# Two-layer graph network on one core: chunks of two rows, messages stored as three bf16 parts, tables cleared during the sort

## The reference, cut to what matters

```python
# x [12500, 32], src, dst [400000] (sorted by dst), edge_attr [400000, 16], edge_weight [400000]
def layer0(h, attr, src, dst):
    edge_mats = (attr @ W_bond + b_bond).reshape(-1, 32, 32)      # one 32x32 matrix per edge
    for _ in range(4):
        msg = einsum('eij,ej->ei', edge_mats, h[dst])             # neighbour: dst
        agg = segment_sum(msg, src, num_segments=12500)           # target: src
        h = gru_cell(agg, h, W_ih, W_hh, b_ih, b_hh)
    return h
def layer1(h, src, dst, edge_weight):
    deg = segment_sum(1, dst);  d = where(deg > 0, rsqrt(deg), 0)
    return segment_sum(h[src] * (d[src] * edge_weight * d[dst])[:, None], dst)
x = x + layer0(relu(layernorm(x)), edge_attr, src, dst)
x = x + layer1(relu(layernorm(x)), src, dst, edge_weight)
```

## Time and profile before

| | us |
|---|---|
| median of three runs | 27440.27 (27435.75 to 27440.9) |
| the profiled execution, its own time | 27437.25 |
| its span, first to last instruction | 27435.5 |
| GpSimd busy | 19769.8, 72% of the span |
| TensorE busy | 12435.2, 45% |
| VectorE busy | 10408.2, 38% |
| ScalarE busy | 4649.9, 17% |
| mean granted clock of TensorE | 0.69 of 2.4 GHz |

### The profile page before, as it was taken

How to read it: one execution, slowest core, us unless ns; L and a number is a source line. 1 busy time by engine, 2 the same in 40 slices (tenths; PEclk the granted TensorE clock), 3 DMA queues, 4 the chain that set the end, 5 groups by cost and what they waited for, 6 DMA issues and landing times. The chain is left out here.

```text
span 27435.5 us, 248655 instructions
## 1 busy us (share of the span) xinstructions
PE 12435.2 (45%) x67848; PEld 9433.8 (34%) x67849; DVE 10408.2 (38%) x18376; ACT 4649.9 (17%) x9970; POOL 19769.8 (72%) x20823
## 2 busy tenths in 40 slices
PE   6666664555555455555455555545555530000004
PEld 5444443344443334334334334333434420000004
DVE  9999995333323323333333333333333330000007
ACT  5333332111111111111111111111111110000004
POOL 2777777777777777777677777777777767777771
PEclk5777776777777677777677777767777765555555
DMA  5333332111111111111111111111111121121113
GB/s 206 93 93 95 92 93 52 29 28 28 28 28 27 28 28 29 29 28 28 26 28 28 28 28 29 27 28 29 28 28 28 28 34 44 45 45 44 44 41 91
DMA packets 1814384, 1246.56 MB, mean 45 GB/s; under 512 B 1182629, under 2 KB 1744754, under 8 KB 1789679
## 3 DMA queue, kind: packets, MB, share of 16 engines
q1 hardware_dynamic: 583936, 850.03, 10.4%
q0 software_dynamic: 666016, 324.92, 8.7%
q10 hardware_dynamic: 564300, 70.11, 1.6%
HBM read 957.69 MB, written 285.80 MB: 45 GB/s over the span
## 5 line engine op out<-in xcount | busy, mean ns | idle before, releaser
L1087 POOL DMA_INDIRECT h_rows<-h_table,rec x13680 | 12906.7, 943 | 4242.1 <-issue 4126.8
L1276 PE MATMUL outer<-a_masked,h_by_quarter 128*128 128x136 f32 x27360 | 5298.9, 366 | 8604.9 <-DVE h_by_quarter L1131 8604.9
L1276 PEld LDWEIGHTS outer<-a_masked,h_by_quarter 128*128 128x128 f32 x27360 | 4985.3, 268 | 9071.7 <-issue 9071.7
L1322 ACT COPY outer_sums<-outer 128x408 f32<-128x408 f32 x4560 | 2276.1, 499 | 14767.5 <-PE outer L1276 14265.7
L1131 DVE TENSOR_TENSOR h_by_quarter<-h_rows,gates 128x1920 f32<-128x1920 f32 x912 | 1964.7, 2154 | 6779.0 <-DMA h_rows<-h_table,rec 6779.0
L1553 POOL DMA_INDIRECT messages_by_bucket<-ms,ix x3420 | 3278.2, 959 | 1063.3 <-issue 1042.5
L843 POOL DMA_INDIRECT edges_by_node<-row,place x3125 | 2992.2, 958 | 958.5 <-issue 954.0
L1241 PE MATMUL msg_psum<-outer_sums,w_bond_blocks 128*128 128x480 f32 x7752 | 3462.5, 593 | 0.0
L1124 DVE TENSOR_TENSOR a_masked<-rec,gates 128x2040 f32<-128x2040 f32 x912 | 2074.7, 2275 | 3656.0 <-PE outer L1276 3635.3
L1241 PEld LDWEIGHTS msg_psum<-outer_sums,w_bond_blocks 128*128 128x128 f32 x7752 | 1547.1, 210 | 1368.1 <-issue 1368.1
L1535 PE MATMUL pgb<-ident_f,gsp_by_chunk_of_tile 128*120 128x128 f32 x228 | 61.6, 426 | 3835.0 <-DVE gsp_by_chunk_of_tile L1473 3835.0
(11 more groups left out here) (275 smaller groups left out, 12623.4 us busy)
## 6 DMA issues: line engine op xcount, KB each, us to landing
h_rows<-h_table,rec POOLq DMA_INDIRECT x13680, 2.4
key_row<-source_keys SPq DMA_DIRECT2D x125, 1600.0 KB
rec<-edges_by_node SPq DMA_DIRECT2D x1140, 157.5 KB, 2.2
low_key_row<-source_low_keys SPq DMA_DIRECT2D x126, 800.0 KB
carry_flags<-carry_flags SPq DMA_DIRECT2D x285, 240.0 KB
mr<-messages_by_bucket SPq DMA_DIRECT2D x220, 264.0 KB, 2.7
messages_by_bucket<-zeros SPq DMA_DIRECT2D x36, 1600.0 KB, 38.0
chunk_sums<-scan_t ACTq DMA_DIRECT2D x912, 60.0 KB, 1.9
```

The source lines that it names most:

```text
L1087: pool.indirect_dma_start(out=hb[j][:, u, :], out_offset=None, in_=ht, in_offset=bass.IndirectOffsetOnAxis(ap=rec[j][:, u, W_DST:W_DST + 1 ...
L1276: last = pe.matmul(pt[(j * NB + g) % RING][:, at:at + KC], hq[j % 2][:, u, :, :].rearrange("p q d -> p (q d)"), am[j % 2][:, u, :, :].rear ...
L1322: act.copy(ts[b][:, :, at:at + w].rearrange("p k (u c) -> p u k c", c=CPT), pt[(j * NB + g) % RING][:, 0:GPB * KC].rearrange("p (u k c) -> ...
```

## The change

**Chunks of two rows.** `CH` = 2: padding is at most one row a node. With `J3` = 16 and `GI` = 2 there are 3232 tiles, 202 iterations and 101 groups. A tile has 16 chunks a quarter, so `am` is 128 x 16 x 17 x 16 and a tile's product has 272 columns; it takes a bank for itself (`GPB` = 1, `NB` = 16), and ScalarE copies each tile by itself. A group has 2 x 256 = 512 columns. The tables by chunk (`st`, `gx`, `gs`, `flags`) have 206,848 rows instead of 109,440. `rec` and `hb` keep four buffers (2 * GI), those of the message block (`rec7`, `ge`, `ms`, `ix`, `fx`) go from four to two. `JD` = 8. The GRU's temporaries share the memory of `am[1]`.

**Spread of h first.** VectorE's group now runs `spread_h(n)` and then `make_a(n+1)`, then the one-hots of `dst`; the scan of two groups ago stays ahead of both.

**Split ahead of the scatter.** The message rows hold three bf16 parts and the key as bf16 pair, 49 words. VectorE and ScalarE split them in the message block; the last block loads them in four buffers and uses them as they are.

**Clearing in slices.** `r3` is still cleared in the counting block. `m2` and `gx` are cleared by two transfers in each iteration of the sort.

```diff
-CH = 4
+CH = 2
-J3 = 15
-GI = 4
-DIV15 = 4370
+J3 = 16
+GI = 2
+TO_ITERATION = 4096
-JD = 15
+JD = 8
+MW = 49
...
-                    for table in (r3, m2, gx):
...
+                    n = clear(sp, (r3,), s_fill)
...
+                    def clear_slice(it):
+                        for flat, width in to_clear:
+                            part = width // IT1
+                            sp.dma_start(flat[:, bass.ds(it * part, part)], zeros[:, 0:part]).then_inc(s_fill2, 16)
...
                         sp.dma_start(di[b][:], dst[e].rearrange("(p u) -> p u", p=P)).then_inc(s_ld[b], 16)
+                        clear_slice(it)
...
-            GPB = 3
+            GPB = 1
...
                             for j in range(GI):
+                                spread_h(n0 + j, b * GI + j, i, j)
                                 if j + 1 < GI:
-                                    make_a(n0 + j + 1, ng, j + 1, (j + 1) % 2)
-                                if past == 2 and j == 2:
-                                    add_degrees(g)
-                                spread_h(n0 + j, ng, j)
-                                if past == 2 and j == 0:
-                                    onehots_of_dst(g)
-                            if b == 0 and not last:
-                                make_a(n0 + GI, ng + 1, 0, 0)
...
+                                    make_a(n0 + j + 1, b * GI + j + 1, i, (j + 1) % 2)
+                                    if past == 2:
+                                        onehots_of_dst(g)
+                                elif b == 0 and not last:
+                                    make_a(n0 + GI, GI, i, 0)
+                            if past == 2:
+                                add_degrees(g)
...
-                                    if g == WEIGH_AT and j == 2 and past == 2:
+                                    if g == WEIGH_AT and j == 1 and past == 2:
                                         pe.wait_ge(s_dd, s * CS + g_)
                                         turn_scan(ng - 2, b)
-                                    if g == 1 and j == 1 and past == 2:
+                                    if g == NB - 2 and j == 0 and past == 2:
                                         count_dst(ng - 2, g_)
...
+                            dve.wait_ge(s_q1, n + 1)
+                            dve.tensor_tensor(prest[j % 2][:], pmsg[j % 2][:], part_of[j][:, :, 0:D], ALU.subtract).then_inc(s_mm, 1)
+                            dve.wait_ge(s_q2, n + 1)
...
+                            dve.tensor_tensor(part_of[j][:, :, 2 * D:3 * D], prest[j % 2][:], part_of[j][:, :, D:2 * D],
+                                              ALU.subtract).then_inc(s_mm, 1)
...
+                            act.copy(part_of[j][:, :, 0:D], pmsg[j % 2][:]).then_inc(s_q1, 1)
...
+                            act.copy(part_of[j][:, :, D:2 * D], prest[j % 2][:]).then_inc(s_q2, 1)
```

More of the change, by code:

```diff
@@ L115, in gnn_program @@
     GW = GI * NT
+    TB = 128
+    NTB = GW // TB
+    assert GW % TB == 0 and NT % TB == 0 and GW <= 512
     USES = ((NGR + 1) // 2, NGR // 2)
@@ L120, in gnn_program @@
     assert T3 * P < BIG and T2 * P < BIG and HB <= P and HB * D <= 7 * 512 and NGR % 2 == 1 and NRUN % 4 == 0
-    assert T3 * DIV15 < 1 << 24 and all(t * DIV15 >> 16 == t // J3 for t in range(T3))
+    assert T3 * TO_ITERATION < 1 << 24 and all(t * TO_ITERATION >> 16 == t // J3 for t in range(T3))
     r3 = nc.dram_tensor("edges_by_node", [T3 * P, W3], F32).ap()
-    m2_all = nc.dram_tensor("messages_by_bucket", [T2 * P + GI * P * J3, D + 1], F32).ap()
+    m2_all = nc.dram_tensor("messages_by_bucket", [T2 * P + GI * P * J3, MW], F32).ap()
     m2 = m2_all[0:T2 * P]
@@ L225, in gnn_program, with clear @@
             s_zero = sem("zeros_made")
-            s_fill = sem("tables_cleared")
+            s_fill = sem("records_cleared")
+            s_fill2 = sem("messages_and_g_cleared")
+            def clear(eng, tables, signal):
+                n = 0
+                for table in tables:
+                    flat = table.rearrange("(p a) w -> p (a w)", p=P)
+                    for at in range(0, flat.shape[1], 3200):
+                        m = min(3200, flat.shape[1] - at)
+                        eng.dma_start(flat[:, at:at + m], zeros[:, 0:m]).then_inc(signal, 16)
+                        n += 1
+                return n
             s_oh_v = sem("onehots_by_vector")
@@ L596, in _ @@
                     sp.dma_start(lo_row[IT1 % 2][:], lo_d_s[0:EI].unsqueeze(0).broadcast_to([P, EI])).then_inc(s_lo[IT1 % 2], 16)
+                    rests = 0
+                    for flat, width in to_clear:
+                        done = width // IT1 * IT1
+                        if done < width:
+                            sp.dma_start(flat[:, done:width], zeros[:, 0:width - done]).then_inc(s_fill2, 16)
+                            rests += 1
                     sp.wait_ge(s_lo[IT1 % 2], 16 * (IT1 // 2 + 1))
+                    sp.wait_ge(s_fill2, 16 * (2 * IT1 + rests))
                 @block.tensor
@@ L1256, in turn_scan @@
                             hold(pe)
-                            for t in range(GI):
-                                last = pe.transpose(px[0:NT, t, :], sc[b][:, t * NT:(t + 1) * NT], ident_f[:])
+                            for t in range(NTB):
+                                last = pe.transpose(px[0:TB, t, :], sc[b][:, t * TB:(t + 1) * TB], ident_f[:])
                             last.then_inc(s_tr, 1)
@@ L1316, in group @@
                                 for g in range(NB):
-                                    if j == 3 and g == 2 and past == 2:
+                                    if g == NB - 3 and j == 1 and past == 2:
                                         store(ng - 2, b, s * USES[b] + i - 1, g_ - 2)
@@ L1533, in spread @@
                         hold(pe)
-                        for j in range(GI):
-                            last = pe.transpose(pgb[0:NT, j, :], gpm[:, j, :], ident_f[:])
+                        gpm_blocks = gpm[:].rearrange("p j (b k) -> p (j b) k", k=TB)
+                        for j in range(NTB):
+                            last = pe.transpose(pgb[0:TB, j, :], gpm_blocks[:, j, :], ident_f[:])
                         last.then_inc(s_gtb, 1)
@@ L1574, in gnn_program, with quads @@
                 sb, pb = alloc(c9)
-                mr = [sb(f"mr{b}", [P, J2, D + 1]) for b in range(2)]
+                mr = [sb(f"mr{b}", [P, J2, MW]) for b in range(4)]
+                rows_b = [m[:].bitcast(BF16) for m in mr]
+                assert IT2 % 4 == 0
+                def quads(engine, body):
+                    with engine.Fori(0, IT2 // 4) as i:
+                        for b in range(4):
+                            body(i * 4 + b, b, i)
                 on = [sb(f"on{b}", [P, J2, P], BF16) for b in range(2)]
-                parts = [sb(f"message_parts{b}", [P, 3, J2, D], BF16) for b in range(2)]
-                rest = [sb(f"message_rest{b}", [P, J2, D]) for b in range(2)]
-                key_n = [sb(f"message_node{b}", [P, J2, 2], BF16) for b in range(2)]
                 zero = sb("zero8", [P, 512])
```

199 lines of the change are left out of this document (89 added, 110 removed).

## The result

The changed kernel takes 28,091.65 us (median of four runs, 28,089.04 to 28,107.68), the kernel before 27,440.54 on the same chip: ratio 1.0238, 95% interval 1.0226 to 1.0251. It is slower by 2.4%, where 26,615 was forecast and 27,030 was the upper end of the range. The profiled execution has a span of 28,091.1 us.

What follows compares the result with a forecast made beforehand. GpSimd's gathers and scatters at a fixed pace were taken to bound the sort, steps and message scatter. -939 + 428 + 25 - 238 - 98 = -822 from 27437 gave 26,615 us, range 26,140 to 27,030.

Steps and rivals of the forecast that it cites:

- The cycle through the first gate: Steps: iteration n's gathers wait until TensorE finished n-2; loop over two iterations 23.9 + D, 20.5 us an iteration, +428 us.
- Bound, gathers saved, duration of a gather: Steps: GpSimd's gathers bound, 752 fewer at 1.248 us, -939 us; each still near 944 ns.
- the rival in which they hide TensorE: Steps: gathers hide TensorE's work entirely, 19.9 against 19.97 us an iteration, 26,187 us; chance 0.2.
- Hand-over 0.3: Steps: TensorE's end to GpSimd's next gather takes 0.3 us, a little above the 0.2 from TensorE to a copy.
- D near 17: Steps: one burst of TensorE takes 14.9 or 15.9 us, 17.9 when started at low clock, mean near 17.
- my mixture: Steps: bursts starting at low and high clock mix, 20.3 to 20.7 us an iteration, 26,450 to 26,780; chance 0.5.
- The second gate is looser: Steps: GpSimd's wait at mid-iteration for half a burst, 3.7 us high or 6.2 low, ends before GpSimd arrives.
- Step ends +25: Ends of the four steps: last burst 5.1 us longer, last product 0.9, 4 x 6 = +25 us.
- Scatter -238: Scatter of messages: 188 fewer scatters at 1.2635 us each, -238 us; new splitting work hidden.
- Final stage -98: Final stage: only one-hots stay on VectorE, 2.09 us an iteration instead of 2.54, -98 us.
- Slower by the ring of banks: Steps: each tile waits for its copy in TensorE's four banks, 23.4 us an iteration, 28,930 us; chance 0.05.
- the port rule: Steps: GpSimd can't write descriptors while VectorE holds their shared port, so longer masking would stretch gathers; prediction argued against it.

Runs made afterwards that it cites:

- without gates: Changed kernel without GpSimd's two waits for TensorE, at the first and ninth gather of an iteration: 26,263.47 us, ratio 0.9573.
- flags late: Changed kernel, SP loading a group's carry flags only after the spread of h in the group's first iteration: 27,373.64 us, ratio 0.9976.
- fillers: Changed kernel with three more unused 512-column matmuls after each burst: 28,010.13 us; with carry flags also loaded after the spread, 26,857.39.
- one at a time: Changed kernel with only GpSimd's wait for TensorE at the first gather kept: 27,557.98 us; only that at the ninth gather kept: 27,811.41.

## Why the prediction was wrong

The loop through the first gate, forecast and measured. The figures are means over the same 384 even iterations of the changed kernel:

| us | forecast | measured |
|---|---|---|
| TensorE's burst (D) | 17 | 16.8 |
| TensorE to GpSimd | 0.3 | 0.8 |
| first to last gather's start | 18.7 | 19.0 |
| last gather's start to the spread | 2.32 | 5.4 |
| spread to TensorE | 2.55 | 2.5 |
| two iterations | 40.9 | 44.5 |

- *Bound, gathers saved, duration of a gather*: right. 752 gathers fewer at 1.248 us; without gates they bound the kernel again, and 26,263 lies near the rival in which they hide TensorE (26,187).
- *The cycle through the first gate*: the mechanism is right, its terms were short. "2.32 us from that gather's start to the spread" was taken from a moment with quiet queues; it is 5.4 where the scan's loads meet it. This is the step that failed most: 3.1 of the 3.6 us that a pair of iterations is longer than forecast. Taking the late landing away (flags late) gives back 718 us and not 404 x 3.1 = 1250, because the loop through the odd iterations, with bursts of 18.2 us (median), then takes over. The earlier trace rows had shown the loads, a DMA share of 0.43 at 10002 to 10004, but not the late landing. In the kernel before the flags were issued 2.7 to 4.5 us ahead of the last gather, 240 KB with no records behind them, and that gather landed in 2.3 us:

```profile
10000.89 0.57 SPq L1056 DMA_DIRECT2D carry_flags<-carry_flags  x1
...
10004.22 0.94 POOL L1087 DMA_INDIRECT h_rows<-h_table,rec  x1 [0.30 <-issue]
...
10006.54 2.15 DVE L1131 TENSOR_TENSOR h_by_quarter<-h_rows,gates 128x1920 f32<-128x1920 f32 x1 [3.50 <-DMA h_rows<-h_table,rec]
```

  No gather of that trace takes more than 3.3 us to land, so 5.4 could not be read from it; what could have been asked is where the loads would fall in the new loop, and how many at once.
- *Hand-over 0.3*: 0.8. I took it from the 0.2 between PE and a copy of ScalarE, which says nothing of GpSimd; and the 0.30 that the earlier trace rows give for 342 waits is GpSimd's usual gap, since those had been met before. Some 0.25 us an iteration.
- *D near 17*: the number came true, the mixture behind it didn't, so it was luck. Slow bursts don't alternate with fast ones on the chain. All 384 even bursts start at 1.2 GHz after 5.9 to 8.3 us idle and take 5.3 to 7.0 us for their first eight tiles, 3.9 at the high clock; with eight weights instead of the nine that I put in, such a burst comes to 14.9 + 2.0 = 16.9. The odd bursts start at 2.4 GHz after 3.3 to 3.7 us idle, but the granted clock falls during the first tiles of 358 of 384, mostly to 5.62 us for eight. An even burst's start and the start of the odd one behind it (granted clock third from the end):

```profile
4672.71:4674.71 2.00, 2.00 (x5) 1.53 (x6) 2.00 (x1) 0.39 (x1) 1.39 (x3) 0.50 0.05 8
...
4693.52:4695.52 2.00, 2.00 (x7) 1.58 (x8) 2.00 (x1) 0.97 (x3) 1.70 (x2) 0.84 0.12 21
4695.52:4697.52 2.00, 2.00 (x6) 1.53 (x5) 2.00 (x1) 0.96 (x3) 1.39 (x3) 0.50 0.06 8
```

  The Trainium skill's page "TensorE: Matmul & The Clock Gate", section "HAM oscillation", by which a loop that waits between bursts pays for each anew, fits here better than my mixture: 742 of the 768 bursts pay. It alone would have given 26,938. With the flags late, fillers regain 0.6 us an iteration.
- *"The second gate is looser"*: wrong by the prediction's own terms: 6.2 + 0.3 + 8.7 + 2.3 + 2.5 = 20.1, above 19.97, and with 0.8 it is 20.8. I compared half a burst with GpSimd's arrival and didn't close the loop over one iteration. The pause at the ninth gather, named as what would prove me wrong, is there in the odd iterations (1.2 to 5.0 us, median 2.8), beside the forecast one of 1.3 us at the first gather of the even ones. Alone this gate costs 1548 us, more than the first (1295), so it isn't the looser one.
- *Step ends +25*: 4 x 13.2 = +53; where the rest comes from wasn't looked into. *Scatter -238*: -173; the pace is (27,587.0 - 23,460.4) / 3231 = 1.277 us instead of 1.2635, and the head of the stage is longer. *Final stage -98*: -92; (28,067.0 - 27,601.7) / 219 = 2.12 us against 2.09. *Clearing 0*: right. VectorE and ScalarE cost nothing in the steps: right.
- *Slower by the ring of banks* (28,930): the sign came true by another mechanism. TensorE doesn't wait for copies: all 4485 us of its idle time before tiles are put down to the spread.
- Of the port rule of the Trainium skill's page "SBUF — State Buffer", section "Who interferes with whom", no sign: gathers take 938 to 982 ns, as before. The section itself lets a `tensor_tensor`, which the masking is, share only the read side with GpSimd, and saw no transfer stall under one; the prediction left that out.

Size of the miss in the steps: 808 x (22.2 - 20.5) is about 1390 us, and 28 at their ends; the other stages add 71. That is 12 us over the miss of 1477.

## What to carry to other kernels

When a change makes iterations shorter or bursts longer, write down every loop that a pacing wait closes, over one iteration as well as over two, and work out for each where the loads fall that it releases. Loads released by one engine's progress move with it: the landing times of the old trace, at most 3.3 us here, don't hold once 592 KB are asked for beside the last gather. A gate that costs nothing while another engine bounds can cost 6.5% when none does (1829 of 28,092 us). Remove all such gates at once before judging one of them: one at a time they seemed to be worth 534 and 281 us. And try it on more than one chip.

## What the runs showed that I had not expected

- A gather of 16 KB lands 2.2 to 2.6 us after its start in quiet queues and 4.8 to 6.1 when 256 KB of flags are issued 0.7 to 2.7 us ahead of it and 336 KB of records behind them.
- Chips differ: the kernel before took 27,436 to 27,478 us on some and 32,978 to 32,990 on two. On the first kind removing GpSimd's gates gains nothing in the kernel before and 6.5% in the changed one; on the second it loses 11% in the kernel before, and the changed kernel itself was never run there. What makes those chips slow isn't settled; GpSimd's and VectorE's instructions are as short there, and their waits are longer.
- GpSimd loses about 1.2 us with nothing in the profile that it waits for, as at 4714.18 in the changed kernel, 147 times and always before the second gather of an iteration, as a rule in every fifth. Its issue time is 234 us over 0.30 for each gather (3750.3 - 11,720 x 0.30), and 61 without gates, where no single gap of this kind is left.
